# Query norms of a linear-attention block: from two selection matmuls to a DRAM scratch

## The reference, cut to what matters

```
q = silu(x @ Wq); k = silu(x @ Wk); v = silu(x @ Wv); z = x @ Wz      # 16 heads of 128
a = x @ Wa; b = x @ Wb                                                # one number a head
q, k, v = causal depthwise convolutions of 4 taps
q, k = rotary embedding
q = q / max(|q|, 1e-12);  k = k / max(|k|, 1e-12)
for s in 0..3:                                                        # 4 lags
    attn = sum_d q[t] * k[t-s] / sqrt(128)
    gate = sigmoid(a[t-s] * b[t])
    out[t] += attn * gate * v[t-s]
out = out * rsqrt(mean(out^2)) * norm_w * silu(z);  s = out @ Wout
y = x + s * silu(ffn(x))                                              # ffn with sign weights
```

## Time and profile before

| | us |
|---|---|
| median of 3 runs | 1412.47 (1412.08 to 1413.2) |
| the profiled execution | 1413.44 |
| its span, first to last instruction | 1411.6 |
| PE busy, in the span | 1377.4 (98%) |
| DVE busy | 1025.6 (73%) |
| ACT busy | 733.3 (52%) |
| POOL busy | 417.2 (30%) |

### The profile page before, as it was taken

The page is one execution under the profiler, slowest core; times in us unless marked ns, Lnnn a source line. Parts: engine busy times, 40 slices in busy tenths (PEclk is TensorE's granted clock), DMA queues, the critical chain, the costliest instruction groups (busy, mean ns, idle before and its releaser), DMA issues. The chain is left out here.

```text
span 1411.6 us, 23209 instructions
## 1 busy us (share of the span) xinstructions
PE 1377.4 (98%) x7048; PEld 1164.4 (82%) x7048; DVE 1025.6 (73%) x1597; ACT 733.3 (52%) x2146; POOL 417.2 (30%) x504
## 2 busy tenths in 40 slices
PE   6999999999999999999999999998899999999998
PEld 4778888888888888888888888886788888888886
DVE  7889999999999999999999999995113322234442
ACT  5655655556655556555565655553554444332221
POOL 6142443434434344444444444432000000000001
PEclk9999999999999999999999999999899999999999
DMA  9123333433344333443334333332431101065454
GB/s 303 38 70 88 90 83 97 99 87 89 79 100 102 75 97 74 104 97 78 93 74 111 89 82 89 82 83 72 137 120 53 45 22 45 25 185 171 142 170 157
DMA packets 103962, 137.60 MB, mean 97 GB/s; under 512 B 11248, under 2 KB 48112, under 8 KB 103664
## 3 DMA queue, kind: packets, MB, share of 16 engines
q1 hardware_dynamic: 94704, 120.28, 29.6%
q0 software_dynamic: 9216, 16.78, 7.0%
HBM read 61.53 MB, written 25.17 MB: 61 GB/s over the span
## 5 line engine op out<-in xcount | busy, mean ns | idle before, releaser
L431 POOL TENSOR_TENSOR rnorm<-norms,neg_half 128x8 f32<-128x8 f32 x64 | 126.2, 1971 | 366.4 <-DVE norms L663 366.4
L556 ACT ACTIVATE bank<-bank 128x128 f32<-128x128 f32 x512 | 133.7, 261 | 86.3 <-PE bank L829 86.3
L638 DVE SCALAR_TENSOR_TENSOR y_v<-u_v,cw_v,y_v 128x512 f32<-128x512 f32 x192 | 172.7, 899 | 6.8
L638 DVE SCALAR_TENSOR_TENSOR y_k<-u_k,cw_k,y_k 128x512 f32<-128x512 f32 x192 | 159.7, 832 | 16.5 <-ACT y_k L536 9.5
L1141 DVE TENSOR_TENSOR hid_lo<-relu,hid_hi 128x512 fp32r<-128x512 f32 x64 | 44.3, 693 | 172.3 <-ACT hid_hi L1087 172.3
L638 DVE SCALAR_TENSOR_TENSOR y_q<-u_q,cw_q,y_q 128x512 f32<-128x512 f32 x192 | 144.2, 751 | 30.0 <-ACT y_q L536 22.3
L1059 POOL TENSOR_TENSOR g_buf<-g_buf,up_raw 128x512 f32<-128x512 f32 x3 | 3.8, 1278 | 402.7 <-DVE g_buf L1162 402.7
L1182 DVE TENSOR_TENSOR hid_lo<-o_raw,hid_hi 128x512 fp32r<-128x512 f32 x64 | 44.3, 692 | 101.4 <-ACT hid_hi L1107 101.4
L1083 ACT ACTIVATE relu<-bank,us_sb 128x512 f32<-128x512 f32 x64 | 44.1, 689 | 121.7 <-PE bank L1222 121.7
L1107 ACT ACTIVATE hid_hi<-o_raw 128x512 fp32r<-128x512 f32 x64 | 40.5, 633 | 121.8 <-PE bank L1252 116.8
L1237 PE MATMUL bank<-down_sign,hid_hi 128*128 128x512 f32 x256 | 99.8, 390 | 0.9 <-DVE hid_lo L1141 0.9
(11 more groups left out here) (173 smaller groups left out, 3560.9 us busy)
## 6 DMA issues: line engine op xcount, KB each, us to landing
swapped_q<-y_q SPq DMA_DIRECT2D x128, 128.0 KB, 2.3
swapped_k<-y_k SPq DMA_DIRECT2D x128, 128.0 KB, 2.3
sq_sum<-out_sq POOLq DMA_DIRECT2D x64, 256.0 KB, 3.4
o_scratch<-o_buf SPq DMA_DIRECT2D x64, 256.0 KB, 2.5
o_raw<-o_scratch SPq DMA_DIRECT2D x64, 256.0 KB, 3.2
raw_q<-in_wq SPq DMA_DIRECT2D x16, 256.0 KB, 3.1
raw_k<-in_wk SPq DMA_DIRECT2D x16, 256.0 KB, 3.6
raw_v<-in_wv SPq DMA_DIRECT2D x16, 256.0 KB, 4.5
```

The lines of the kernel that those rows point to most:

```text
L431: nc.gpsimd.tensor_tensor(rnorm[:, g1 % 2, :], norms[:, g1 % 2, :], neg_half[:, 0:2 * BC], ALU.pow).then_inc(root_done, 1)
L556: last = nc.scalar.activation(block_of, block_of, ACT.Square, accum_out=norms[:, g1 % 2, i * BC + b:i * BC + b + 1])
L638: nc.vector.scalar_tensor_tensor(y[n][:, g % 2, :], u[n][:, g % 2, i:i + CH], cw[n][:, bass.ds(h * TAPS + i, 1)], y[n][:, g % 2, :], ALU.m ...
```

## The change

POOL now takes the floor of the norms itself, and its root goes to `rnorm` as before. SP stores the 4 query columns of `rnorm` (128 partitions x 4) to a DRAM scratch `rq_scratch[group]`, the first 4 tokens of the following block once more as an appendix of the same rows, and the first 4 tokens of the group as appendix of the group before. One step later SP reads for each partition p a window of 8 consecutive token rows, beginning with 4 * floor(p / 4), into `rq_win`. POOL masks it with two 0/1 triangles (`window`), adds both halves, and multiplies by `gate_k` into `gates`. The two matmuls, the three `rq_parts` instructions, the constant `sel_r` and DVE's L663, L711 and L715 are gone. POOL's wait for `gate_done` moves from its prologue to just before the first `gate_k`. SP issues the three stores before the swaps, behind a wait for the root, and the load behind the swaps. POOL makes the gates after the weight splits and ahead of the DMA of the squares. The core of the diff:

```diff
@@ SP, step @@
+                if at := back(h, g, 1):
+                    g1 = at[1]
+                    wait(sp, root_done, c)
+                    own = rnorm[:, g1 % 2, 0:BC]
+                    sp.dma_start(rq_scratch[g1, 0:P, :], own).then_inc(rq_stored, 16)
+                    sp.dma_start(rq_scratch[g1, P:P + LAGS, 0:BC - 1], own[0:LAGS, 1:BC]).then_inc(rq_stored, 16)
+                    first = own[0:LAGS, 0:1] if g1 > 0 else rot["q"][0:LAGS, S:S + 1]
+                    sp.dma_start(rq_scratch[(g1 - 1) % G, P:P + LAGS, BC - 1:BC], first,
+                                 allow_slow_non_contiguous=True).then_inc(rq_stored, 16)
...
+                if at := back(h, g, 2):
+                    g2 = at[1]
+                    wait(sp, rq_stored, 48 * (c if back(h, g, 1) else c - 1))
+                    runs = bass.AP(tensor=rq_scratch.tensor, offset=rq_scratch[g2].offset,
+                                   ap=[[LAGS * BC, P // LAGS], [0, LAGS], [1, WIN * BC]])
+                    sp.dma_start(rq_win[:, g2 % 2, :, :].rearrange("p j b -> p (j b)"), runs).then_inc(rq_in, 16)
@@ POOL, prologue and step @@
-            pool.wait_ge(gate_done, 2)
...
+                    wait(pool, norms_done, c)
+                    pool.sem_inc(norms_seen, 1)
+                    nc.gpsimd.tensor_scalar(norms[:, g1 % 2, :], norms[:, g1 % 2, :], NORM_FLOOR, None, ALU.max
+                                            ).then_inc(floor_done, 1)
                     wait(pool, floor_done, c)
+                    wait(pool, rq_stored, 48 * (c - 2))
                     nc.gpsimd.tensor_tensor(rnorm[:, g1 % 2, :], norms[:, g1 % 2, :],
                                             neg_half[:, 0:2 * BC], ALU.pow).then_inc(root_done, 1)
                     wait(pool, root_done, c)
-                    wait(pool, rq_done, c - 1)
-                    spread = (rnorm[:, g1 % 2, 0:BC][:, :, None].broadcast_to([P, BC, LAGS]),
-                              period[:, None, :].broadcast_to([P, BC, LAGS]))
-                    nc.gpsimd.tensor_tensor(rq_x[:, :, :], *spread, ALU.mult).then_inc(rq_spread, 1)
-                    wait(pool, rq_picked, c - 3)
-                    nc.gpsimd.tensor_tensor(rq_parts[:, blocks, 0, :], *spread, ALU.mult).then_inc(rq_spread, 1)
-                    wait(pool, rq_spread, 2 * c)
-                    nc.gpsimd.tensor_tensor(rq_parts[:, blocks, 1, :], rq_x[:, :, :],
-                                            rq_parts[:, blocks, 0, :].bitcast(fp32), ALU.subtract
-                                            ).then_inc(rq_done, 1)
-                    wait(pool, gates_done, c - 3)
+                    if is_start(h, g - 1):
+                        pool.wait_ge(gate_done, 2)
...
+                if at := back(h, g, 2):
+                    g2 = at[1]
+                    win = rq_win[:, g2 % 2, :, :]
+                    wait(pool, rq_in, 16 * (c - 1))
+                    nc.gpsimd.tensor_tensor(win, win, window[:, :, None].broadcast_to([P, WIN, BC]), ALU.mult
+                                            ).then_inc(rq_masked, 1)
+                    wait(pool, rq_masked, c - 1)
+                    nc.gpsimd.tensor_tensor(rq_own[:, :, :], win[:, 0:LAGS, :], win[:, LAGS:WIN, :], ALU.add
+                                            ).then_inc(rq_joined, 1)
+                    wait(pool, rq_joined, c - 1)
+                    wait(pool, rnorm_done, c - 1)
+                    wait(pool, gated, c - 2)
+                    nc.gpsimd.tensor_tensor(gates[:, :, :], rq_own[:, :, :].rearrange("p r b -> p b r"),
+                                            gate_k[:, g2, :, :], ALU.mult).then_inc(gates_done, 1)
@@ ACT, prologue @@
-            act.wait_ge(const_in, 16)
-            nc.scalar.activation(sel_r[:, :, :].rearrange("p a n -> p (a n)"), const[:, P:3 * P], ACT.Copy
-                                 ).then_inc(sel_done, 1)
@@ DVE, step @@
-                if at := back(h, g, 1):
-                    g1 = at[1]
-                    wait(dve, norms_done, c)
-                    nc.vector.tensor_scalar(norms[:, g1 % 2, :], norms[:, g1 % 2, :], NORM_FLOOR, None, ALU.max
-                                            ).then_inc(floor_done, 1)
...
-                    wait(dve, rq_picked, c - 1)
-                    parts = bank_rq[:, 0:2 * BC * LAGS].rearrange("p (b k r) -> p b k r", b=BC, k=2)
-                    nc.vector.tensor_reduce(gates[:, :, :], parts.rearrange("p b k r -> p b r k"),
-                                            mybir.AxisListType.X, ALU.add).then_inc(rq_joined, 1)
-                    wait(dve, rq_joined, c - 1)
-                    wait(dve, rnorm_done, c - 1)
-                    nc.vector.tensor_tensor(gates[:, :, :], gates[:, :, :], gate_k[:, g2, :, :], ALU.mult
-                                            ).then_inc(gates_done, 1)
@@ PE, step @@
-                    wait(pe, rq_done, c - 1 + ahead)
-                    wait(pe, gates_done, c - 2)
-                    if is_start(h, g - 2):
-                        pe.wait_ge(sel_done, 1)
-                    own = rq_parts[:, g2 * BC:(g2 + 1) * BC, :, :].rearrange("p b k r -> p (b k r)")
-                    after = rq_parts[:, g2 * BC + 1:(g2 + 1) * BC + 1, :, :].rearrange("p b k r -> p (b k r)")
-                    nc.tensor.matmul(bank_rq[:, 0:2 * BC * LAGS], sel_r[:, 0, :], own, start=True, stop=False)
-                    nc.tensor.matmul(bank_rq[:, 0:2 * BC * LAGS], sel_r[:, 1, :], after, start=False, stop=True
-                                     ).then_inc(rq_picked, 1)
```

More of the change, by code:

```diff
@@ L64, in gated_recurrent_block_kernel @@
     SCALE = float(D) ** -0.5
-    C_ID, C_SEL, C_HALO, C_BAND, C_PER = 0, P, 2 * P, 3 * P, 3 * P + BW
+    C_ID, C_SEL, C_HALO, C_BAND, C_PER, C_WIN = 0, P, 2 * P, 3 * P, 3 * P + BW, 3 * P + BW + LAGS
+    WIN = 2 * LAGS
     o_scratch = nc.dram_tensor("o_scratch", [HD, S], fp32).ap()
+    rq_scratch = nc.dram_tensor("rq_scratch", [G, P + LAGS, BC], fp32).ap()
     def wait(eng, sem, count):
@@ L123, in gated_recurrent_block_kernel @@
         period = const[:, C_PER:C_PER + LAGS]
+        window = const[:, C_WIN:C_WIN + WIN]
         banks = [top.enter_context(nc.psum_tensor(f"bank{i}", [P, 512], fp32)) for i in range(4)]
@@ L155, in attention @@
     (fp32, f32r, ALU, ACT, P, S, HID, KT, H, D, CH, G, BC, NB, LAGS, HALO, TAPS, BW, AB, SCALE, LN_EPS,
-     NORM_FLOOR, sb, sem, wait) = (
+     NORM_FLOOR, WIN, sb, sem, wait) = (
         env[n] for n in ("fp32", "f32r", "ALU", "ACT", "P", "S", "HID", "KT", "H", "D", "CH", "G", "BC", "NB",
[L158 to L162, removed]
+                         "LAGS", "HALO", "TAPS", "BW", "AB", "SCALE", "LN_EPS", "NORM_FLOOR", "WIN", "sb",
+                         "sem", "wait"))
+    (const, neg_half, x_hi, x_lo, sq_sum, ident, sel_own, sel_next, band, period, window, banks, pair, banks2, cw,
+     gate0, raw, w_hi, w_lo, raw_in, whi_done, wlo_done, w_slice, nw_sb, us_sb, o_scratch, up_raw, down_raw, ones,
+     ones_set, o_stored, rq_scratch) = (
         env[n] for n in ("const", "neg_half", "x_hi", "x_lo", "sq_sum", "ident", "sel_own", "sel_next", "band",
-                         "period", "banks", "pair", "banks2", "cw", "gate0", "raw", "w_hi", "w_lo", "raw_in",
+                         "period", "window", "banks", "pair", "banks2", "cw", "gate0", "raw", "w_hi", "w_lo", "raw_in",
                          "whi_done", "wlo_done", "w_slice", "nw_sb", "us_sb", "o_scratch", "up_raw",
-                         "down_raw", "ones", "ones_set", "o_stored"))
+                         "down_raw", "ones", "ones_set", "o_stored", "rq_scratch"))
     sum_squares, SQ_EARLY = env["sum_squares"], env["SQ_EARLY"]
@@ L264, in attention @@
         rnorm_done = sem("rnorm_done", ctx)
-        rq_spread = sem("rq_spread", ctx)
-        rq_done = sem("rq_done", ctx)
-        rq_picked = sem("rq_picked", ctx)
+        norms_seen = sem("norms_seen", ctx)
+        rq_stored = sem("rq_stored", ctx)
+        rq_in = sem("rq_in", ctx)
+        rq_masked = sem("rq_masked", ctx)
         rq_joined = sem("rq_joined", ctx)
-        sel_done = sem("sel_done", ctx)
         scores_done = sem("scores_done", ctx)
@@ L369, in _ @@
                 env["load_ffn_weights"](sp, i)
+            sp.wait_ge(cleared, 5)
             schedule(sp, step)
@@ L421, in _ @@
             pool.wait_ge(const_in, 16)
-            pool.wait_ge(gate_done, 2)
-            pool.wait_ge(cleared, 6)
+            pool.wait_ge(cleared, 5)
             def step(h, g):
@@ L509, in _ @@
             act.wait_ge(small_in, 16 * 5)
-            act.wait_ge(cleared, 6)
+            act.wait_ge(cleared, 5)
             def split_hi(n, h, c):
@@ L791, in _ @@
             project_ab(3)
-            pe.wait_ge(cleared, 6)
+            pe.wait_ge(cleared, 5)
             def turn_v(g1, c):
@@ L1300, in shape_constants @@
         (p[:, None] % lags) == np.arange(lags)[None, :],
+        np.arange(lags)[None, :] >= (p[:, None] % lags),
```

(1 more changed line is left out.)

10 lines of the change are left out of this document (4 added, 6 removed).

## The result

The changed kernel takes 1395.18 us (median of 4 runs, 1394.53 to 1395.44) against 1412.53 for the kernel before in the same series (1412.08 to 1413.20): a ratio of 0.9875 with a 95% interval of 0.9861 to 0.9889. The profiled execution took 1395.03 with a span of 1393.2, so 1.83 lies around it.

A forecast was written before the change was run, and what follows sets the result against it. PE was taken to bound the kernel in the steady steps. Matmuls -8.5, start -6.2 and end +3.0 sum to -11.7, from 1412.47 to 1400.8 us; range 1397.8 to 1407.8.

The forecast's parts named there:

- What bounds the kernel: Attention stage, steady steps: PE sets the pace, busy 800 of 800 us; DVE has about 1.0 us of slack a step.
- The two matmuls: PE, ahead of the score products: removing both selections gains 0.14 us a step, 8.5 in 61 steps; lower bound 2.4.
- Rival 2: PE's selections: almost free, the score products' weight load takes their place; gain 2.4 instead of 8.5, 1406.9 us; chance 0.06.
- DVE, nothing: DVE loses three instructions, 0.52 us a step; buys nothing by itself, slack rises from 1.0 to about 1.4.
- POOL and the DRAM path in the steady steps, nothing: Steady steps: POOL's new work and DRAM landings of 2.2 us stay hidden, by 0.7 us in the tightest step.
- Rival 4: L720 on DVE: gates come too late in every step, slower than before; 1481 us at a landing of 5.5; chance 0.09.
- The start: Attention stage's start: POOL's wait for the gates moves behind the first root, k starts 6.2 us earlier; bounds 3.0 to 6.5.
- Rival 3: Stage's start not won: clock still falls (1404.0 us) or swaps pushed so PE meets another wait (1407.0); chance 0.07.
- The end: Attention stage's end, nothing overlapping: DRAM trips move the last DMA of the squares 3.0 us later; upper bound 9.3.
- Rival 1: Stage's end: the DRAM round trips cost their upper bound, 9.3 us, giving 1407.1 us; chance 0.10.
- Rival 5: Stores wait on a root that waits on a load, one loop across steps; counted under Rival 4, no chance of its own.

## Why the prediction was too small

**What bounds the kernel** was read rightly: PE at 800 of 800 in the steady steps, before and after. More work on DVE changed nothing, more work on PE came through in full.

**The two matmuls, -8.5: the mechanism was right, this term was mis-sized, and it makes the miss.** It measured 14.2 in 60 steps, 0.236 a step instead of 0.14. The step that failed is the price drawn from "PE could start the score products where it starts L889 ... their weight load then lies under a 512-column product". The load does lie there now (601.38), but the 0.14 counts only the move of the start of the score products to L889's place; their end was left to move along by the same 0.14, as if their own length didn't depend on what stands ahead of them. But the long product covers one weight load, and before it covered that of L889; the load of the first score product then lay open, 0.09 in their length of 0.99. Removing the pair gives 0.03 + 0.11 between its starts, and this 0.09 behind it: two open loads of 0.112. The runs that show it are the pair put back (13.2 of 14.2), the pair elsewhere (the 0.1 moves to the k products) and the 32 weight columns (the 0.11 falls to 0.03, the 0.09 stays). The comparison that I made, z to L889 and v to L813, was one of starts alone; the sums over values followed to the next group's start with and without their narrow pair, 0.89 against 0.81, would have given 0.14 + 0.08 = 0.22, 13.4 us in 61 steps, and a forecast of 1395.9. The rows on record hinted at it: eight products of 132 columns take 1.15 behind the pair and 1.06 behind a long product.

I named the lower bound of this term (0.04) and no upper one. That is why the range missed too: its low end took the 8.5 as the most that the pair could give.

Rival 2 (the matmuls nearly free, 1406.9) is refuted. By the spacing of the Trainium skill, "TensorE: Matmul & The Clock Gate", section "Wait — 56ns, not 53.3ns?", which the prediction weighed, the term would have been about 3 us; the trace has 14. The measured 0.03 between the first two starts agrees with it, and so does the 0.03 behind weights of 32 columns; behind the second selection with its 128 it is 0.11.

**DVE, nothing:** right, by the run with the three put back. Its slack was mis-sized, without harm here: I had it rise from 1.0 to 1.4 us a step, taking off the full 0.52; by the windows it is 61.6 us in 56 steps, 1.1, since the busy time fell by 0.33 only and the step by 0.236.

**POOL and the DRAM path in the steady steps, nothing:** right for PE. The page of the kernel after gives the load's landing, the list of waits (engine, line, waited for: us in total, times, longest) DVE's:

```profile
DVE coef L730 <- POOL gates L478: 18.6, 19, 6.8
```

The median landing of the 64 loads is 2.03 us (1.99 to 3.03); I had taken 2.2. In the 19 waits DVE stands for 18.6 us, and 6.84 + 3.90 of that are the two at the end. In the steady steps it waits 0.13 us on average out of its slack, nearly all of it as 0.52 in one step of four, and there it isn't the DRAM path:

```profile
574.53 1.35 POOL L423 TENSOR_TENSOR wlo_z<-raw_z,whi_z 128x512 fp32r<-128x512 f32 x1 [7.84 <-ACT whi_z L539]
575.84 0.69 POOL L470 TENSOR_TENSOR rq_win<-rq_win,const 128x32 f32<-128x32 f32 x1
...
577.59 0.71 DVE L730 TENSOR_TENSOR coef<-bank,gates 128x528 f32<-128x528 f32 x1 [0.52 <-POOL gates L478]
```

The window had landed at 573.35, but POOL stands in the weight split of z, which waits for ACT, and takes the window only at 575.84. My search for the tightest step had looked at SP's issues alone; of the splits ahead of the gates I had named those of group 3, not this one.

The three stores are issued at 951.55, 951.94 and 952.31, and the load that waits for all of them at 953.47: so the first, 4 numbers a partition, lands in under 1.92 us, the last, 4 numbers in all, in under 1.2.

**Rival 4, the gates too late, 1481:** didn't come about, and its thresholds hold as far as they were tried. I put DVE's waits at a landing beyond 2.95 and PE's loss at 4.35. At 4.0 DVE waits 0.58 a step, 0.8 in two steps of four that had no wait at 2.0, and PE loses only in three of the first five of the 60. The waits at 2.0 are those of the z split. Where PE begins to lose in every step wasn't reached by a run.

**The start, -6.2:** right in size and reason. From c = 1 to c = 4 it is -6.65. The move of the wait alone gives -6.20 there, and the other 0.45 are the pairs of two steps. Timeline of the kernel after:

```profile
68.90 0.59 POOL L457 TENSOR_TENSOR gate_k<-gate,rnorm 128x16 f32<-128x16 f32 x1 [15.55 <-DVE gate L721]
...
73.01 1.07 PE L898 MATMUL bank<-rot_q,rot_k 128*128 128x132 f32 x8
...
79.34 0.71 DVE L730 TENSOR_TENSOR coef<-bank,gates 128x528 f32<-128x528 f32 x1 [0.19 <-POOL gates L478]
```

POOL still stands for the gates, 15.55 us, but now its first root is behind it. PE starts the scores at 73.01 (forecast 72.82), k at 77.54 (77.44), and the first gates reach DVE at 79.34 (79.4), with 0.19 of waiting. This is worth as much as it is because PE's gap of 2.96 us had dragged 7 us of the low level behind it; in the run with the wait moved alone there is neither. Rival 3 would have had 3.0 or nothing here.

**The end, +3.0:** measured +2.03, with errors of both signs inside:

```profile
952.31 0.29 SPq L364 DMA_DIRECT2D rq_scratch<-rnorm  x1
...
953.47 0.55 SPq L378 DMA_DIRECT2D rq_win<-rq_scratch  x1
...
956.51 0.71 DVE L730 TENSOR_TENSOR coef<-bank,gates 128x528 f32<-128x528 f32 x1 [6.84 <-POOL gates L478]
...
957.36 2.10 PE L898 MATMUL bank<-rot_q,rot_k 128*128 128x132 f32 x8 [2.03 <-DVE coef L730]
...
958.31 0.76 SPq L378 DMA_DIRECT2D rq_win<-rq_scratch  x1
...
962.39 0.71 DVE L730 TENSOR_TENSOR coef<-bank,gates 128x528 f32<-128x528 f32 x1 [3.90 <-POOL gates L478]
...
968.17 0.86 POOL L484 DMA_DIRECT2D sq_sum<-out_sq  x1 [4.45 <-ACT out_sq L602]
```

The root is done at 951.52 (0.4 later behind c = 64 than reckoned), the first gate product follows 5.0 after it instead of 6.7, mostly because the stores have landed 0.9 after the last issue ended (952.60) instead of 2.0; the second follows 5.9 after the first instead of 5.1, because this load, issued 0.4 behind the store of `o_buf` (957.90), lands after 3.03 instead of 2.2 (in the run with two loads the one behind that store takes 3.06 and the same load again 1.96); the last DMA of the squares then comes 5.8 behind it instead of 6.3, with the one before it landing after 3.87 instead of the 5.4 of before. 0.4 - 1.7 + 0.8 - 0.5 is about -1.0. Rival 1 (9.3 instead of 3.0) is refuted, and the price is real: with the matmuls in the two closing steps the end is 2.92 shorter.

**Rival 5:** the loop across steps closes in time, as shown by the unchanged 14.29 with 2 us more in it.

## What to carry to other kernels

Cost a group of matmuls from the start of what stands before it to the end of what stands behind it, and count the weight loads that no long product covers: here each short matmul with weights of its own added one (0.11 us at 128 weight columns), and changing the order took none away. Give every term of a sum a bound on the gain's side too, above all one that was derived from where things could start. A trip through DRAM was free for PE where a step's slack covered it and cost time in the steps that drain the pipeline, so there the old way can be kept. Before calling a step the tightest, go through the queue of every engine on the way, not only that of the DMAs.

## What the hardware showed beyond that

- Two matmuls with 32 moving columns and 128 x 128 weights cost PE 0.22 to 0.25 us, in either place; with 128 moving columns the step was the same, with 32 weight columns it fell by 0.08, and each further matmul costs 0.10 (two: 0.193).
- A store of 16 bytes a partition and the load behind it landed in under 1.92 and in 2.0 us at the stage's end; right behind a 256 KB store the same load took 3.03. The Trainium skill, "DMA: Bandwidth & Descriptors", section "Latency and other measured facts", gives about 0.8 us as the least for a trip to HBM; the trace agrees as far as it goes, since neither transfer is shown to be faster than that.
- At the stage's end the granted clock is at its low level from 956.7 to 984.0, behind the waits of PE, and eight score products last 2.10 us there against 1.07. The stretch is longer than before's 17.1 us (983.1 to 1000.2), and yet the time from the next block's start to the end of the span is the same within 0.1 us.
